# Attention of a vision layer: value matmuls over two heads of a key head, probabilities of 16 heads buffered

## The chip, the cores and the metric

One core of one Trainium2 chip runs the whole kernel as one program. The metric is the device time of one execution in microseconds, the median over runs. The kernel before takes 955.35 us (three runs, 954.17 to 960.56).

## What is computed

Thirty-two images of 256 tokens go through one layer: patches are embedded, an attention block with 16 query heads and 4 key heads follows, then a gated feed-forward block whose weights and inputs are rounded to 8 bits. Cut to what matters here:

```python
q = (x @ wq).reshape(Bx, Sx, 16, 16)
k = (x @ wk).reshape(Bx, Sx, 4, 16)
v = (x @ wv).reshape(Bx, Sx, 4, 16)
q, k = _apply_rope(q, cos, sin), _apply_rope(k, cos, sin)
# head h uses the key and value head h % 4
scores = jnp.einsum('bshd,bthd->bhst', q, k) * scale
scores = jnp.where(causal[None, None, :, :], scores, -jnp.inf)
attn = jax.nn.softmax(scores, axis=-1)
out = jnp.einsum('bhst,bthd->bshd', attn, v).reshape(Bx, Sx, Dx)
return out @ wo
```

Since head h uses value head h % 4, heads 4g to 4g + 3 (a group, g = 0 to 3) use the four value heads once each, and head kv of group g and head kv of group g + 1 share one.

## The kernel before

The kernel has three stages: attention over images (up to about 770 us), then gate and up, then down. Only the first is touched. It is written engine by engine, with its order laid down by hand in one function `step(x)` for each engine, and run for x from -2 to 32: six steps written out, twelve loop rounds of two images, and the rest written out. Step x works on four images at once: patch, normalisation and projection of x + 2, row maxima of x + 1, scores, exponentials and values of x, output projection of x - 1. Each engine goes through its own step in order, and engines meet only at semaphores.

In step x TensorE (PE) does, for image x:
- `score_pair(x, i)`, i = 0 to 7 (L547, L549): transposed scores of two heads into PSUM; the causal structure leaves three blocks of 128x128 a head.
- `attend(x, g)`, g = 0 to 3 (L563, L567): the value product of the four heads of group g. The values (`v_aug`, 32 columns for each value head, with a column of ones for the row sums) are the stationary operand, so that four value heads occupy the four column groups of the array; the probabilities move through, 256 columns for the first key block and 128 for the second, all fp32. The result goes to half of an `o_bank`, two groups to a bank.

ScalarE (ACT) takes each pair of scores to probabilities in `exp_pair` (L865), into `probs`, a buffer of eight heads, and copies a full `o_bank` out in `o_copy` (L873). GpSimd (POOL) zeroes the upper triangle of the diagonal blocks in `mask` (L1013), once for each pair. VectorE (DVE) reduces row maxima of image x + 1 (`reduce_pair`, L1223) as PE delivers them (`unit_pair`, L525 and L532), and works on the normalisation (L1244 to L1264), on `xn_low` (L1297), `max_turned` (L1214) and on the output side.

What waits for what around the change: attend(x, g) waits for masks up to 2g + 1 (`masked`), and for `o_copied` when it begins a bank; exp_pair(x, i) for even i waits for `pv_done`, the attend that last read its half of `probs`; o_copy waits for the two attends of its bank; `values` (L818) for the attends of the image that used the same `v_aug`. In PE's step the order is: patch 0, attend(x - 1, 3), stack_turn 1, patch 1, score 0, stack_turn 2, max_turn 0 and 1, score 1, o_turn 0, unit 0, score 2, o_turn 1, x_turn, stack_turn 0, score 3, unit 1, attend(x, 0), project 0, score 4, unit 2, project 1, score 5, on_turn, unit 3, attend(x, 1), score 6, unit 4, out_project, score 7, unit 5, attend(x, 2). In matmul lines: patch is L454, stack_turn L509, max_turn L491, o_turn L578, x_turn L467, project L479, on_turn L587, out_project L598.

POOL's step is: power, masks 0 to 3, x_low (L1051), mask 4, rotate_cross (L1032), mask 5, rotate (L1021), mask 6, add_rotated (L1046), mask 7, power. rotate_cross waits for both `projected` (L811) of ACT, which wait for project 0 and 1 of PE.

Of the kernel before, what the change touches and what calls it, by code (L numbers as in the profile page):

```python
# [26 lines left out]
P = 128  # L27
# [3 lines left out]
D = 256  # L31
# [89 lines left out]
def vit_layer(nc, x_t, w_emb, w_qkv, w_o, w_gate, w_up, w_down, clips, rope, eye, tri, out):  # L121
    with ExitStack() as ctx:
# [64 lines left out]
        probs = part(8 * 4 * P).rearrange("p (h k s) -> p h k s", h=8, k=4)  # L187
        diagonals = probs.rearrange("p h (a b) s -> p (h a) b s", a=2)[:, :, 0, :]
# [23 lines left out]
        gate_q = ffn[:, 2 * IM * D:5 * IM * D // 2].bitcast(BF16).rearrange("p (m e) -> p m e", m=IM)  # L212
        up_q = ffn[:, 5 * IM * D // 2:3 * IM * D].bitcast(BF16).rearrange("p (m e) -> p m e", m=IM)
        down_n = part(DC * I).rearrange("p (c i) -> p c i", c=DC)
        down_q = part(DC * I, BF16).rearrange("p (c i) -> p c i", c=DC)
        w_inv = part(2 * IM + DC)
        down_diag = part(DC * P).rearrange("p (c h) -> p c h", c=DC)
# [207 lines left out]
        def _(pe):  # L425
# [127 lines left out]
            def attend(x, g):  # L553
                pe.wait_ge(masked, x.n * 8 + (2 * g + 2))
                if g == 0:
                    pe.wait_ge(v_ready, x.n + 1)
                if g % 2 == 0:
                    wait(pe, o_copied, x.n * 2 + (g // 2 - 1))
                cols = (g % 2) * TOKENS
                b = o_bank[g // 2]  # L560
                v = v_aug[x.parity]
                for kv in range(KV):
                    pe.matmul(b[32 * kv:32 * kv + 32, cols:cols + TOKENS], v[:, 0, kv, :],  # L563
                              probs[:, 4 * (g % 2) + kv, 0:2, :], start=True, stop=False,
                              skip_group_check=True)
                for kv in range(KV):
                    mm = pe.matmul(b[32 * kv:32 * kv + 32, cols + P:cols + TOKENS], v[:, 1, kv, :],  # L567
                                   probs[:, 4 * (g % 2) + kv, 2, :], start=False, stop=True,
                                   skip_group_check=True)
# [64 lines left out]
            def step(x):  # L634
# [4 lines left out]
                if w:  # L639
                    attend(x + -1, 3)  # L640
# [30 lines left out]
                if X:  # L671
                    attend(x, 0)
# [16 lines left out]
                if X:  # L689
                    attend(x, 1)  # L690
# [11 lines left out]
                if X:  # L702
                    attend(x, 2)
# [78 lines left out]
        def _(act):  # L782
# [31 lines left out]
            def values(x):  # L814
                y = x + 1
                act.wait_ge(read["qkv"], y.n * 2 + 2)
                wait(act, pv_done, y.n * 4 - 4)
# [42 lines left out]
            def exp_pair(x, i):  # L860
                act.wait_ge(scored, x.n * PAIRS_S + (i + 1))
                if i % 2 == 0:
                    wait(act, pv_done, x.n * 4 + (i // 2 - 1))
                o = 2 * i % 8
# [691 lines left out]
```

## Time and profile before

| | |
|---|---|
| median of three runs | 955.35 us |
| profiled execution, its device time | 954.55 us |
| its span, first to last instruction | 952.8 us |
| mean granted TensorE clock | 0.971 |
| PE busy | 820.2 us, 86% |
| DVE busy | 732.7 us, 77% |
| ACT busy | 621.8 us, 65% |
| POOL busy | 520.0 us, 55% |
| L563, 1024 instructions | 82.7 us |
| L567, 1024 instructions | 51.9 us |
| L1223, 192 instructions | 235.1 us |

Busy time is the time in which at least one instruction of the group runs. Matmuls overlap on PE, so the distance from one start to the next tells more about their cost than their durations. A wait in brackets is idle time of the engine ahead of a row, with the engine, tile and line that ended it.

### The profile page before, as it was taken

Reading aid. Unit: us, or ns where it says so; the run is one execution under the profiler, and the core shown is the slowest. Engines: PE = TensorE matmul, PEld = TensorE weight load, DVE = VectorE, ACT = ScalarE, POOL = GpSimd, SP = SyncE. Lnnn points to the kernel's source line nnn. Section 1 sums busy time; section 2 is a strip of 40 time slices with the busy share of each in tenths; the row PEclk is TensorE's granted clock in tenths of the full one; section 3 lists DMA queues with packets and bytes.
Section 4 is the critical chain, followed back from the end, with each engine's and each line's share of the span. In section 5 each row is a group of like instructions: output and inputs, shape, how many; then the busy total and the mean of one; then the engine's idle time right before and its main releaser. Section 6 shows DMA issues by size and latency. Waiting matters only on the chain. (4 is left out here: it accounts for less than half of the span.)

```text
span 952.8 us, 25805 instructions
## 1 busy us (share of the span) xinstructions
PE 820.2 (86%) x8942; PEld 480.8 (50%) x8942; DVE 732.7 (77%) x1309; ACT 621.8 (65%) x972; POOL 520.0 (55%) x545
## 2 busy tenths in 40 slices
PE   2689999999999999999999999999997849997775
PEld 2345555555555555555555555555554433332443
DVE  5856777777777777777777777777777758999898
ACT  3266666666666666666666666666676537886664
POOL 1456666555666566666666665655565326884000
PEclk9789999999999999999999999999999888998899
DMA  7000111111111111111111111111100011322488
GB/s 268 29 2 2 51 57 51 41 39 39 39 39 39 39 39 39 39 39 39 39 39 39 39 50 49 55 39 39 39 13 12 13 43 36 56 44 67 148 261 251
DMA packets 50052, 54.59 MB, mean 57 GB/s; under 512 B 18912, under 2 KB 45280, under 8 KB 50016
## 3 DMA queue, kind: packets, MB, share of 16 engines
q1 hardware_dynamic: 50016, 54.11, 18.8%
q8 instruction: 22, 0.36, 0.1%
q14 instruction: 14, 0.11, 0.0%
HBM read 33.13 MB, written 16.78 MB: 52 GB/s over the span
## 5 line engine op out<-in xcount | busy, mean ns | idle before, releaser
L1223 DVE TENSOR_REDUCE act_all<-pair 128x8 f32<-128x1024 f32 x192 | 235.1, 1225 | 98.6 <-PE pair L532 98.0
L865 ACT ACTIVATE act_all<-pair 128x768 f32<-128x768 f32 x256 | 207.9, 812 | 133.2 <-PE pair L549 133.2
L1013 POOL TENSOR_SCALAR_AFFINE_SELECT act_all<-act_all 128x512 f32<-128x512 f32 x256 | 162.6, 640 | 100.5 <-ACT act_all L865 100.4
L1056 POOL TENSOR_TENSOR act_all<-act_all 128x2 f32<-128x2 f32 x64 | 60.8, 950 | 210.5 <-DVE act_all L1256 139.9
L454 PE MATMUL pair<-act_all 128*128 128x256 f16 (+1 forms) x960 | 118.4, 277 | 9.4 <-DVE act_all L1158 9.4
L857 ACT ACTIVATE act_all<-pair 128x1024 f16<-128x1024 f16 x64 | 65.7, 1027 | 76.7 <-PE pair L509 76.7
L454 PEld LDWEIGHTS pair<-act_all 128*128 128x128 f16 (+1 forms) x960 | 91.5, 99 | 26.6 <-issue 15.4
L525 PE MATMUL pair<-act_all,eye_b 128*128 128x512 bf16 x256 | 78.5, 389 | 26.6 <-DVE act_all L1223 25.9
L563 PE MATMUL pair<-act_all 128*32 128x256 f32 x1024 | 82.7, 395 | 1.3 <-POOL act_all L1013 1.3
L1051 POOL TENSOR_TENSOR act_all<-act_all 128x1280 f16<-128x1280 f32 x31 | 80.9, 2611 | 1.3 <-ACT act_all L795 1.3
L532 PEld LDWEIGHTS pair<-act_all 32*128 32x128 f16 x1536 | 43.4, 93 | 67.3 <-issue 66.0
L532 PE MATMUL pair<-act_all 32*128 32x128 f16 x1536 | 76.6, 218 | 0.8 <-DVE act_all L1223 0.8
L547 PE MATMUL pair<-act_all 64*128 64x256 f16 x512 | 73.1, 282 | 4.3 <-ACT act_all L857 2.2
L479 PE MATMUL pair<-act_all 128*128 128x384 f16 x384 | 75.6, 335 | 1.5 <-DVE act_all L1297 1.5
L974 ACT ACTIVATE ffn<-pair,gate_scale 128x512 f32<-128x512 f32 x96 | 60.9, 654 | 16.2 <-PE pair L730 9.1
L770 PE MATMUL pair<-wd_t,act_all 128*128 128x256 bf16 (+1 forms) x384 | 46.7, 279 | 20.4 <-ACT act_all L997 20.4
L1032 POOL TENSOR_TENSOR act_all<-act_all 128x320 f32<-128x320 f32 x64 | 53.9, 865 | 17.4 <-ACT act_all L811 17.4
L549 PE MATMUL pair<-act_all 64*128 64x128 f16 x512 | 56.7, 218 | 0.0
L730 PE MATMUL pair<-ffn,wg_t 128*128 128x512 bf16 x160 | 49.1, 389 | 7.3 <-DMA ffn<-ffn 6.2
L578 PE MATMUL pair<-act_all 128*128 128x128 f32 x256 | 42.1, 288 | 14.7 <-DVE act_all L1214 13.9
L509 PE MATMUL pair<-act_all 128*128 128x128 f16 x640 | 52.8, 222 | 1.0 <-DVE act_all L1280 0.8
L1113 POOL TENSOR_TENSOR act_all<-ffn 128x512 f32<-128x512 f32 x32 | 40.7, 1273 | 22.1 <-ACT ffn L962 22.1
(133 smaller groups left out, 1625.9 us busy)
## 6 DMA issues: line engine op xcount, KB each, us to landing
act_all<-x_t SPq DMA_DIRECT2D x32, 640.0 KB, 4.0
out<-act_all SPq DMA_DIRECT2D x32, 256.0 KB, 2.2
ffn<-out SPq DMA_DIRECT2D x16, 512.0 KB, 4.6
out<-ffn SPq DMA_DIRECT2D x16, 512.0 KB, 3.2
act_all<-w_down SPq DMA_DIRECT2D x1, 704.0 KB, 8.4
act_all<-w_emb SPq DMA_DIRECT2D x1, 640.0 KB, 4.0
ffn<-w_gate SPq DMA_DIRECT2D x1, 640.0 KB, 7.1
ffn<-w_up SPq DMA_DIRECT2D x1, 640.0 KB, 7.6
```

Source lines behind the costliest of these rows:

```text
L454: mm = pe.matmul(b[:, 0:D], xs[0:k, sx, c, tb * P:(tb + 1) * P], we[0:k, sw, c, :], start=(c == 0 and (sx, sw) == PARTS[0]), stop=(c == KC ...
L479: mm = pe.matmul(b[:, 0:QKV_COLS], xn_t[:, sx, c, tb * P:(tb + 1) * P], wqkv[:, sw, c, :], start=(c == 0 and (sx, sw) == PARTS[0]), stop=( ...
L525: pe.matmul(max_bank[j], eye_b[:, :], tri_b.rearrange("p (a t) -> p a t", a=1).to_broadcast([P, GROUPS, P]), start=True, stop=False, skip_ ...
L532: mm = pe.matmul(max_bank[j][:, g * P:(g + 1) * P], max_op[rows, g, qt * P:(qt + 1) * P], max_op[rows, 4, kt * P:(kt + 1) * P], start=(qt ...
L547: pe.matmul(b[:, 0:TOKENS], k[rows, kp, 0:P], q[rows, i, :], start=True, stop=True)
L563: pe.matmul(b[32 * kv:32 * kv + 32, cols:cols + TOKENS], v[:, 0, kv, :], probs[:, 4 * (g % 2) + kv, 0:2, :], start=True, stop=False, skip_ ...
L857: act.activation(q_op[y.parity][:, 4 * (k - 1):4 * k, :].rearrange("p g t -> p (g t)"), max_bank[k - 1][:, :].bitcast(FP16), ACT.Copy).the ...
L865: act.activation(probs[:, o:o + 2, 0:3, :].rearrange("p h k s -> p h (k s)"), pair[1][:, :].rearrange("p (h c) -> p h c", h=2)[:, :, 0:3 * P],
L974: act.activation(silu[m % 3][:, 0:cols], bank[2 + m % 3][:, 0:cols], ACT.Silu, scale=gate_scale[:, m:m + 1]).then_inc(silu_ready, 1)
L1013: pool.affine_select(out=p, in_=p, pattern=[[0, 4], [1, P]], compare_op=ALU.is_ge, fill=0.0, base=0, channel_multiplier=-1).then_inc(maske ...
L1051: pool.tensor_tensor(x_parts[v.parity][:, 1], xt[v.parity], x_parts[v.parity][:, 0], ALU.subtract).then_inc(x_low_ready, 1)
L1223: dve.tensor_reduce(to.rearrange("p (g k) -> p k g", g=GROUPS)[:, first:first + 2, :], pair[2][:, :].rearrange("p (k g t) -> p k g t", k=2 ...
```

## The change

`probs` becomes two buffers of eight heads, so all 16 heads of an image have a place: pairs 0 to 3 in the first, pairs 4 to 7 in the second, which lies in the `ffn` tile. attend(x, half) now handles eight heads: each matmul takes the same value head for two groups, 512 columns for the first key block and 2 x 128 for the second, and fills a whole `o_bank`. It is called twice an image: half 0 where attend(x, 1) stood, half 1 where attend(x - 1, 3) stood. The calls for attend(x, 0) and attend(x, 2) are gone. The waits follow: `pv_done` counts two for an image instead of four, attend waits for four or eight masks, exp_pair waits for pv_done only at i = 0 and 4. The feed-forward weights' small buffers change places with the part of `ffn` that is now used.

```diff
-        probs = part(8 * 4 * P).rearrange("p (h k s) -> p h k s", h=8, k=4)
+        probs = [t.rearrange("p (h k s) -> p h k s", h=8, k=4) for t in (part(8 * 4 * P), ffn[:, 0:8 * 4 * P])]
...
-        gate_q = ffn[:, 2 * IM * D:5 * IM * D // 2].bitcast(BF16).rearrange("p (m e) -> p m e", m=IM)
-        up_q = ffn[:, 5 * IM * D // 2:3 * IM * D].bitcast(BF16).rearrange("p (m e) -> p m e", m=IM)
+        gate_q, up_q = (part(IM * D, BF16).rearrange("p (m e) -> p m e", m=IM) for _ in range(2))
...
-            def attend(x, g):
-                pe.wait_ge(masked, x.n * 8 + (2 * g + 2))
-                if g == 0:
+            def attend(x, half):
+
+                pe.wait_ge(masked, x.n * 8 + (4 * half + 4))
+                if half == 0:
                     pe.wait_ge(v_ready, x.n + 1)
-                if g % 2 == 0:
-                    wait(pe, o_copied, x.n * 2 + (g // 2 - 1))
-                cols = (g % 2) * TOKENS
-                b = o_bank[g // 2]
+                wait(pe, o_copied, x.n * 2 + (half - 1))
+                b = o_bank[half]
                 v = v_aug[x.parity]
+                p = probs[half].rearrange("p (g h) k s -> p g h k s", g=2)
                 for kv in range(KV):
-                    pe.matmul(b[32 * kv:32 * kv + 32, cols:cols + TOKENS], v[:, 0, kv, :],
-                              probs[:, 4 * (g % 2) + kv, 0:2, :], start=True, stop=False,
+                    pe.matmul(b[32 * kv:32 * kv + 32, :].rearrange("p (g t) -> p g t", g=2), v[:, 0, kv, :],
+                              p[:, :, kv, 0:2, :].rearrange("p g k s -> p g (k s)"), start=True, stop=False,
                               skip_group_check=True)
                 for kv in range(KV):
-                    mm = pe.matmul(b[32 * kv:32 * kv + 32, cols + P:cols + TOKENS], v[:, 1, kv, :],
-                                   probs[:, 4 * (g % 2) + kv, 2, :], start=False, stop=True,
+                    mm = pe.matmul(b[32 * kv:32 * kv + 32, :].rearrange("p (g t) -> p g t", g=2)[:, :, P:TOKENS],
+                                   v[:, 1, kv, :], p[:, :, kv, 2, :], start=False, stop=True,
                                    skip_group_check=True)
...
-                    attend(x + -1, 3)
+                    attend(x + -1, 1)
...
-                if X:
-                    attend(x, 0)
                 if z:
                     project(x, 0)
...
-                    attend(x, 1)
+                    attend(x, 0)
                     score_pair(x, 6)
...
-                if X:
-                    attend(x, 2)
...
-                wait(act, pv_done, y.n * 4 - 4)
+                wait(act, pv_done, y.n * 2 - 2)
...
-                if i % 2 == 0:
-                    wait(act, pv_done, x.n * 4 + (i // 2 - 1))
-                o = 2 * i % 8
-                act.activation(probs[:, o:o + 2, 0:3, :].rearrange("p h k s -> p h (k s)"),
+                if i % 4 == 0:
+                    wait(act, pv_done, x.n * 2 + (i // 4 - 1))
+                o = 2 * (i % 4)
+                act.activation(probs[i // 4][:, o:o + 2, 0:3, :].rearrange("p h k s -> p h (k s)"),
...
-                act.wait_ge(pv_done, img.n * 4 + (2 * b + 2))
+                act.wait_ge(pv_done, img.n * 2 + (b + 1))
```

First place: PE's queue in the middle of a step, from unit_pair(x, 1) to the second project. L525 and L532 are unit_pair, L563 and L567 attend, L479 project, L547 and L549 score_pair. Before:

```order
L525 MATMUL pair<-act_all,eye_b 128x512 [waits unit_reduced]
L525 MATMUL pair<-act_all,eye_b 128x512
L532 MATMUL pair<-act_all 128x128 x8
L563 MATMUL pair<-act_all 32x256 [waits o_copied,v_ready,masked]
L563 MATMUL pair<-act_all 32x256 x3
L567 MATMUL pair<-act_all 32x128 x4
L479 MATMUL pair<-act_all 128x384 [waits x_t_read]
L479 MATMUL pair<-act_all 128x384 x5
```

The same place now:

```order
L525 MATMUL pair2<-act_all,eye_b 128x512 [waits unit_reduced]
L525 MATMUL pair2<-act_all,eye_b 128x512
L532 MATMUL pair2<-act_all 128x128 x8
L479 MATMUL pair0<-act_all 128x384 [waits x_t_read]
L479 MATMUL pair0<-act_all 128x384 x5
```

attend(x, 0) is gone from here, with its waits, and project follows unit_pair at once.

Second place: PE's queue from unit_pair(x, 5) over the end of the step to stack_turn 1 of the next (L454 is patch 0, L509 stack_turn). Before:

```order
L532 MATMUL pair<-act_all 128x128 x8
L563 MATMUL pair<-act_all 32x256 [waits o_copied,masked]
L563 MATMUL pair<-act_all 32x256 x3
L567 MATMUL pair<-act_all 32x128 x4
L454 MATMUL pair<-act_all 128x256 [waits x_low_ready,x_high_ready,on_t_read]
L454 MATMUL pair<-act_all 128x256 x14
L563 MATMUL pair<-act_all 32x256 [waits masked]
L563 MATMUL pair<-act_all 32x256 x3
L567 MATMUL pair<-act_all 32x128 x4
L509 MATMUL pair<-act_all 128x128 [waits max_ready,stack_high]
```

The same place now:

```order
L532 MATMUL pair2<-act_all 128x128 x8
L454 MATMUL pair0<-act_all 128x256 [waits x_low_ready,x_high_ready,on_t_read]
L454 MATMUL pair0<-act_all 128x256 x14
L563 MATMUL pair3<-ffn,act_all 32x512 [waits o_copied,masked]
L563 MATMUL pair3<-ffn,act_all 32x512 x3
L567 MATMUL pair3<-ffn,act_all 32x2x128 x4
L509 MATMUL pair2<-act_all 128x128 [waits max_ready,stack_high]
```

The attend ahead of patch is gone, and the one behind it has matmuls of 512 and 2 x 128 columns and reads the second buffer.

Third place: PE's queue from unit_pair(x, 3) to unit_pair(x, 4). Now:

```order
L532 MATMUL pair2<-act_all 128x128 [waits unit_reduced]
L532 MATMUL pair2<-act_all 128x128 x7
L563 MATMUL pair3<-act_all 32x512 [waits o_copied,v_ready,masked]
L563 MATMUL pair3<-act_all 32x512 x3
L567 MATMUL pair3<-act_all 32x2x128 x4
L547 MATMUL pair1<-act_all 128x256 [waits exp_done]
```

Nothing has moved past anything here; the attend between them is the doubled one, where before it had 256 and 128 columns.

## Rows read from the trace of the kernel before

**Rows 1.** Busy time in a window: length, then PE, PEld, DVE, ACT, POOL, clock, DMA, GB/s
```profile
84.50:717.21 632.71, 584.50 (x7057) 354.34 (x7057) 480.66 (x953) 429.38 (x701) 393.26 (x420) 1.00 0.12 40
```
**Rows 2.** Waits from 90 to 720 us: who for whom, total us, times, longest
```profile
ACT act_all L865 <- PE pair L549: 113.2, 107, 1.8
...
PE pair L525 <- DVE act_all L1223: 20.5, 56, 0.5
...
PE pair L467 <- DVE act_all L1264: 14.9, 28, 0.5
...
PE pair L578 <- DVE act_all L1214: 12.8, 28, 0.8
```
**Rows 3.** Timeline of PE in one image: start, us, engine, line, shapes, count [wait]
```profile
401.00 0.60 PE L525 MATMUL pair<-act_all,eye_b 128*128 128x512 bf16 x2 [0.46 <-DVE act_all L1223]
401.54 0.40 PE L532 MATMUL pair<-act_all 32*128 32x128 f16 x8
401.86 0.64 PE L563 MATMUL pair<-act_all 128*32 128x256 f32 x8
402.32 0.40 PE L567 MATMUL pair<-act_all 128*32 128x128 f32 x8
402.65 1.15 PE L479 MATMUL pair<-act_all 128*128 128x384 f16 x6
...
403.85 0.22 PE L549 MATMUL pair<-act_all 64*128 64x128 f16 x2
404.00 0.40 PE L532 MATMUL pair<-act_all 32*128 32x128 f16 x8
404.33 1.15 PE L479 MATMUL pair<-act_all 128*128 128x384 f16 x6
...
407.50 0.22 PE L549 MATMUL pair<-act_all 64*128 64x128 f16 x2
407.99 0.61 PE L525 MATMUL pair<-act_all,eye_b 128*128 128x512 bf16 x2 [0.27 <-DVE act_all L1223]
...
413.94 0.64 PE L563 MATMUL pair<-act_all 128*32 128x256 f32 x8
```
**Rows 4.** Timeline of PE inside one attend, its passes, from narrow windows
```profile
406.60 0.42 PE L563 MATMUL pair<-act_all 128*32 128x256 f32 x4
...
406.84 0.40 PE L563 MATMUL pair<-act_all 128*32 128x256 f32 x4
407.05 0.40 PE L567 MATMUL pair<-act_all 128*32 128x128 f32 x8
```
**Rows 5.** Timeline of DVE and POOL in the same image
```profile
401.25 0.69 DVE L1297 TENSOR_TENSOR act_all<-pair,act_all 128x512 f16<-128x512 f32 x1 [0.31 <-ACT act_all L801]
...
401.97 1.23 DVE L1223 TENSOR_REDUCE act_all<-pair 128x8 f32<-128x1024 f32 x1
...
402.09 0.63 POOL L1013 TENSOR_SCALAR_AFFINE_SELECT act_all<-act_all 128x512 f32<-128x512 f32 x1 [2.23 <-ACT act_all L865]
...
406.09 1.68 POOL L1032 TENSOR_TENSOR act_all<-act_all 128x320 f32<-128x320 f32 x2 [0.21 <-ACT act_all L811]
...
406.71 1.23 DVE L1223 TENSOR_REDUCE act_all<-pair 128x8 f32<-128x1024 f32 x1 [1.04 <-PE pair L532]
...
411.91 0.64 POOL L1013 TENSOR_SCALAR_AFFINE_SELECT act_all<-act_all 128x512 f32<-128x512 f32 x1
```
**Rows 6.** Timeline of PE in the last three images
```profile
728.82 0.64 PE L563 MATMUL pair<-act_all 128*32 128x256 f32 x8 [0.34 <-POOL act_all L1013]
...
740.48 0.40 PE L532 MATMUL pair<-act_all 32*128 32x128 f16 x8 [0.36 <-DVE act_all L1223]
...
755.80 1.08 PE L563 MATMUL pair<-act_all 128*32 128x256 f32 x8
...
766.40 0.64 PE L563 MATMUL pair<-act_all 128*32 128x256 f32 x8 [0.92 <-POOL act_all L1013]
```
**Rows 7.** Durations of one line in the whole run: ns least/median/greatest
```profile
L1013 POOL TENSOR_SCALAR_AFFINE_SELECT act_all<-act_all x256: 627/635/954, 59.0 to 765.7; 128x512 f32<-128x512 f32 x128
```

More of the change, by code:

```diff
@@ L184, in vit_layer @@
         v_aug = [part(TB * KV * 32).rearrange("p (b h d) -> p b h d", b=TB, h=KV) for _ in range(2)]
-        probs = part(8 * 4 * P).rearrange("p (h k s) -> p h k s", h=8, k=4)
-        diagonals = probs.rearrange("p h (a b) s -> p (h a) b s", a=2)[:, :, 0, :]
+        probs = [t.rearrange("p (h k s) -> p h k s", h=8, k=4) for t in (part(8 * 4 * P), ffn[:, 0:8 * 4 * P])]
+        diagonals = [p.rearrange("p h (a b) s -> p (h a) b s", a=2)[:, :, 0, :] for p in probs]
         o_sb = part(GROUPS * TOKENS).rearrange("p (g t) -> p g t", g=GROUPS)
@@ L211, in vit_layer @@
         up_n = ffn[:, IM * D:2 * IM * D].rearrange("p (m e) -> p m e", m=IM)
-        gate_q = ffn[:, 2 * IM * D:5 * IM * D // 2].bitcast(BF16).rearrange("p (m e) -> p m e", m=IM)
-        up_q = ffn[:, 5 * IM * D // 2:3 * IM * D].bitcast(BF16).rearrange("p (m e) -> p m e", m=IM)
+        gate_q, up_q = (part(IM * D, BF16).rearrange("p (m e) -> p m e", m=IM) for _ in range(2))
         down_n = part(DC * I).rearrange("p (c i) -> p c i", c=DC)
-        down_q = part(DC * I, BF16).rearrange("p (c i) -> p c i", c=DC)
+        down_q = ffn[:, 4096:4096 + DC * I // 2].bitcast(BF16).rearrange("p (c i) -> p c i", c=DC)
         w_inv = part(2 * IM + DC)
-        down_diag = part(DC * P).rearrange("p (c h) -> p c h", c=DC)
+        down_diag = ffn[:, 4096 + DC * I // 2:4096 + DC * (I // 2 + P)].rearrange("p (c h) -> p c h", c=DC)
         ones = part(P)
@@ L1011, in mask @@
                 fence(pool)
-                p = diagonals[:, 4 * (r % 4):4 * (r % 4) + 4, :]
+                p = diagonals[r // 4][:, 4 * (r % 4):4 * (r % 4) + 4, :]
                 pool.affine_select(out=p, in_=p, pattern=[[0, 4], [1, P]], compare_op=ALU.is_ge,
```

## The prediction

> **What bounds the kernel now.** I start with the busy sums, because they say which engine can set the pace at all. From L525 at 84.50 to the L525 that stands 28 images later the period is 632.71/28 = 22.60 us an image, and TensorE (PE) is busy for 584.50 of the 632.71 us, 92%, at a granted clock of 1.00, that is 2.4 GHz; VectorE (DVE) is busy 76%, ScalarE (ACT) 68%, GpSimd (POOL) 62% [rows 1]. So PE's own work is the period, apart from about 1.7 us of waits an image. The list of waits says where these are: four places, each waiting for DVE, in each image alike. L525 waits for the reduction L1223 twice (20.5 us over 28 images, 0.73 an image: 0.46 at 401.00 and 0.27 at 407.99), L467 for L1264 (0.53) and L578 for L1214 (0.46) [rows 2, 3]. The reader is to see in the timeline of PE that everything else stands back to back. Work taken off PE therefore counts in full as long as no other engine is late at the next wait, and work added just ahead of a wait is free up to the size of that wait. That is the whole argument; what follows is a walk through one image with a clock in hand, from L525 at 401.00 on.
>
> **The price of one attend.** Before, an attend starts at 401.86 and the next work (L479) starts at 402.65: 0.79 us. Its first half (L563 to L567) is 0.46, the second, with the way out, 0.33 [rows 3]. Inside, the trace shows two passes for each matmul (x8 for four written, 1024 for 512 in the run): passes of 256 columns start at 406.60 and 406.84, and L567 starts at 407.05 [rows 4]. So the second pass takes 0.21 us for 256 columns, with four column groups of the array side by side. Four passes of streaming (256, 256, 128, 128 columns) are then 0.21 + 0.21 + 0.11 + 0.11 = 0.64, and 0.15 is fixed for one attend. Is the fixed part really lost with the attend, or does it stay with the neighbours? L532 takes 0.32 before an attend (401.54 to 401.86) and 0.33 before L479 (404.00 to 404.33) [rows 3]: the neighbour costs the same without it, so a removed attend gives back its 0.79.
>
> **The doubled attend.** No row shows 512 fp32 columns in one matmul. From below its price is streaming alone, 1.28; from above twice the old attend, 1.58. I take 1.43 = 2 x 0.64 + 0.15, because what the two pieces of 0.21 and 0.24 us show is a pace by columns with one small start. The output of L567 now has two runs of 128 columns, and its input has two runs far apart; for that I add nothing, and the upper end stands for it. The TensorE page of the Trainium skill ("TensorE: Matmul & The Clock Gate", Back-to-back issue gap) gives a warm matmul a fixed cost of only about 2.5 ns beyond its columns; by that rule merging saves next to nothing, a doubled attend costs nearly the upper end, and the sum would be that of the first rival below. No row here shows that figure by itself, and the 0.15 us above speaks against its use here.
>
> **The walk.** Times are those of the image shown.
>
> First, attend(x, 0) leaves the place behind unit_pair(x, 1). project (L479) could start at 401.86 instead of 402.65, but it needs xn_low, which DVE ends at 401.25 + 0.69 = 401.94 [rows 5]; DVE's result is used about 0.05 later, so 402.00. Gain 0.65. The next unit_pair would start at 403.35; it needs the reduction of 401.97 + 1.23 = 403.20, used at 403.25 [rows 5]. Nothing is lost, but only 0.10 is left.
>
> Second, attend(x, 1) becomes the doubled attend(x, 0): +0.64. It asks for masks 0 to 3, the last of which ends at 402.09 + 0.63 = 402.72, over 3 us before it [rows 5]. Behind it come score_pair(x, 6) and then L525, which before waited: after an L549 the next work comes 0.15 later when nothing is late (403.85 to 404.00); this one started at 407.50, so PE was ready at 407.65 and began at 407.99, 0.34 late [rows 3]. The reduction it waited for starts when unit_pair(x, 3) is through (406.71), ahead of the attend, and doesn't move against it [rows 5]. The extra 0.64 thus fills the 0.34 and costs 0.30. After two steps PE is 0.35 ahead.
>
> Third, attend(x, 2) leaves the end of the step: 0.79 gained. Fourth, the old attend(x, 3) at 413.94 is now the doubled attend(x, 1): 0.64 lost. It starts at 413.94 - 0.35 - 0.79 = 412.80 and asks for mask 7. It ends at 411.91 + 0.64 = 412.55 [rows 5]. POOL works on end from mask 3 to there, with one wait of 0.21 ahead of L1032, for the second projected [rows 5]. PE brings that 0.65 earlier, so the 0.21 goes and mask 7 ends at 412.34: 0.4 of slack where there was 1.4.
>
> The sum for an image: -0.65 + 0.30 - 0.79 + 0.64 = -0.50 us; 0.30 of it is the fixed part of two attends, 0.20 is what the moved places do with waits. I go on with 0.49, as the second decimals of the starts allow no more. The rest of the way (stack_turn, the second patch, both embedded, L1244, L1214, L1264, the reduction) hangs on PE's stack_turn and patch by the waits in the code and moves as one piece, so the three waits of 0.46, 0.53 and 0.46 stay. ACT and DVE see the same work. ACT loses one wait on pv_done in two; none of these was ever the last, since every wait of L865 in the list is for PE's L549 [rows 2]. The moved weight buffers and masks of another tile change no instruction's size, so 0.
>
> How many images? Steps with a patch behind them: images 0 to 28, 29 x 0.49 = 14.2 us.
>
> The last three images differ: no patch separates the last attends. At 728.82 PE already waits 0.34 for POOL's mask, and at 766.40 it waits 0.92 [rows 6]; now 1.43 us of attend stand behind that mask instead of 0.79. Image 29: the mask comes 0.2 earlier and the attend ends 0.64 later, +0.44. Image 30: the place freed by attend(x, 0) is swallowed by a reduction (wait of 0.36 [rows 6]), the two doubled attends cost 0.37 and 0.4: +0.8. Image 31: partly at the lower of PE's two clocks (L563 shows 1.08 for 0.64 at 755.80 [rows 6]) I take -0.5 for attend(x, 0), whose place the exponentials' wait takes over in part, +1.2 for the first doubled attend at that clock (0.64 x 1.08/0.64, rounded up for the way out) and +0.64 for the second, behind the wait for the mask: +1.3. These three are the roughest numbers of the sum. Together +2.5, with 1 and 3.5 as its ends.
>
> The profiled execution: 954.55 - 14.2 + 2.5 = 942.85. It lies 0.80 below the median of the runs shown, 955.35, so the forecast in median terms is 943.7 us, 1.2% less. (About 1% is what a measurement of this kernel can tell from no change.)
>
> **Rivals.**
> *Merging saves no time on PE.* If the fixed 0.15 belongs to each matmul's columns after all, a doubled attend costs 1.58, and an image gives -0.65 + 0.45 - 0.79 + 0.79 = -0.20: 5.8 us, less a tail of 3.2 (2.5 and five attends of 0.15). That is 954.55 - 2.6 + 0.80 = 952.7, within 1%. For it speaks that 512 fp32 columns stand in no row; against it the 0.21 of the pure pass [rows 4]. The rule cited above from the Trainium skill ("TensorE: Matmul & The Clock Gate") comes out here.
>
> *The first gap isn't closed.* With attend(x, 0) gone nothing covers the chain reduction, xn_low, reduction. Its slack is 0.10; if DVE, or ACT's L801 ahead of xn_low, is 0.25 us later than in the rows, the first gain is 0.40 to 0.50 and the image gives about 0.27 us: 29 x 0.27 - 2.5 = 5.3, so 954.55 - 5.3 + 0.80 = 950. For it: 0.10 is thin. Against it: PE's waits for DVE repeat from image to image, with longest ones of 0.5 us where the mean is 0.46 and 0.53 [rows 2].
>
> *Slower: mask 7 comes too late.* attend(x, 1) holds back PE, and patch, stack_turn and ACT's L857 queue behind it. It decides from the point where mask 7 ends 0.4 + 0.49 = 0.9 us later than computed. L1013 lasts 635 ns as a rule and 954 at most [rows 7]; were all five masks of the chain that long, mask 7 would come 1.6 later, PE would wait 1.2, and an image would be 0.7 us longer than before: +20 us with the tail on top, 978. Only something that slows POOL in every image would do it, and the 0.21 ahead of L1032 shows POOL with a little room.
>
> *The change doesn't do what it says* isn't open: the halved count of attends is written down in the order.
>
> **From cases to numbers.** The forecast has 0.6 (own range 940 to 946, down to the sum without the tail and the clock's scatter), the merge without a saving 0.2, the open first gap 0.14, the late mask 0.06. Faster by over 1% (below 945.8) is the first case, 0.6; within 1% the next two, 0.34; slower 0.06. The range goes from 940 to 953 and leaves out the last case and a little on the low side.
>
> **What the new profile would show.** L563 would have 512 instructions of 512 columns; the distance from its start to the next work would be 1.43 (right) or 1.58 (the first rival). L479 would show a wait of about 0.14 for L1297. The wait of 0.27 at L525 would be gone, the three of 0.45 to 0.52 would be there. The doubled attend in front of stack_turn would show no wait for POOL; one there is the slower rival. The period would be 22.1 us. A period of 22.3 to 22.4 with an attend of 1.43 would mean that I've missed a wait.

## The result and the profile after

The changed kernel takes 945.65 us in the median of 15 runs (944.16 to 950.83); the kernel before takes 954.49 us (15 runs). The ratio is 0.9912, with a 95% interval of 0.9893 to 0.9930: 0.9% faster, where 1.2% had been forecast (943.7 us), inside the range of 940 to 953, and by the ratio just inside the band of 1% to which the forecast had given a chance of 0.34, against 0.6 for more. Counted by its border of 945.8 us, which was worked out from the median of 955.35, it lies 0.15 us on the other side. A second set of five runs, beside the last experiments, gave 945.15 us and a ratio of 0.9904 (0.9889 to 0.9919). The profiled execution takes 945.95 us with a span of 944.2, against 954.55 and 952.8.

The changed kernel has other line numbers from ScalarE's part on: L1223 is now L1219 (the reduction), L1297 is L1293 (xn_low), L1264 is L1260, L1214 is L1210, L1013 is L1009 (mask), L1032 is L1028, L865 is L861, L857 is L853. PE's lines are the same.

First the busy time in a window that answers to [rows 1]: length, then PE, PEld, DVE, ACT, POOL, granted clock, DMA share, GB/s.

```profile
85.48:706.59 621.11, 575.85 (x6160) 331.34 (x6161) 480.59 (x953) 429.36 (x701) 392.88 (x420) 1.00 0.13 41
```

The same 28 images take 621.11 us instead of 632.71, 22.18 instead of 22.60 an image. DVE, ACT and POOL are busy for what they were busy before, to 0.5 us; PE has lost 8.65 us of work, and 2.95 us of idle time have gone too. The waits (who for whom, total, times, longest; 90 to 720 us) answer to [rows 2]:

```profile
ACT ffn L861 <- PE pair L549: 103.4, 86, 1.4
...
PE pair L467 <- DVE act_all L1260: 15.1, 28, 0.5
...
PE pair L525 <- DVE act_all L1219: 13.0, 28, 0.5
PE pair L578 <- DVE act_all L1210: 12.7, 28, 0.8
...
PE pair L479 <- DVE act_all L1293: 4.2, 26, 0.2
```

L525 now waits once an image, not twice (28 for 56), and L479 has a new wait of 0.16. The timeline of one image (start, us, engine, line, shapes, count, wait) answers to [rows 3] and [rows 5]:

```profile
396.17 0.60 PE L525 MATMUL pair<-act_all,eye_b 128*128 128x512 bf16 x2 [0.46 <-DVE act_all L1219]
396.42 0.69 DVE L1293 TENSOR_TENSOR act_all<-pair,act_all 128x512 f16<-128x512 f32 x1 [0.31 <-ACT act_all L797]
396.71 0.40 PE L532 MATMUL pair<-act_all 32*128 32x128 f16 x8
...
397.26 1.14 PE L479 MATMUL pair<-act_all 128*128 128x384 f16 x6 [0.16 <-DVE act_all L1293]
...
398.60 0.40 PE L532 MATMUL pair<-act_all 32*128 32x128 f16 x8
...
400.87 0.40 PE L532 MATMUL pair<-act_all 32*128 32x128 f16 x8
...
401.19 1.06 PE L563 MATMUL pair<-act_all 128*32 128x512 f32 x8
...
402.07 0.61 PE L567 MATMUL pair<-act_all 128*32 128x256 f32 x8
...
402.62 0.28 PE L547 MATMUL pair<-act_all 64*128 64x256 f16 x2
...
402.89 0.61 PE L525 MATMUL pair<-act_all,eye_b 128*128 128x512 bf16 x2
...
406.85 0.63 POOL L1009 TENSOR_SCALAR_AFFINE_SELECT ffn<-ffn 128x512 f32<-128x512 f32 x1
...
408.06 1.06 PE L563 MATMUL pair<-ffn,act_all 128*32 128x512 f32 x8
...
409.49 0.62 PE L509 MATMUL pair<-act_all 128*128 128x128 f16 x8
...
418.33 0.60 PE L525 MATMUL pair<-act_all,eye_b 128*128 128x512 bf16 x2 [0.47 <-DVE act_all L1219]
```

The reader is to see four things. The doubled attend takes 402.62 - 401.19 = 1.43 and 409.49 - 408.06 = 1.43 us. From L525 to the L532 of unit_pair(x, 2) it is now 2.43 us; it was 3.00 [rows 3]: 0.57 gained. From unit_pair(x, 3) at 400.87 to L525 at 402.89 it is 2.02 with no wait; 0.30 dearer than before. And mask 7 ends at 407.48, the attend that needs it starts at 408.06.

### The profile page after: what moved, and what is told of

Its sections match the earlier page's. It is cut to its first block and busy times, and to the rows that moved or that the text cites. A ratio compares the mean times of both kernels' runs of the same rounds, so it can differ in the third digit from the quotient of the medians.

```text
span 944.2 us, 23705 instructions
## 1 busy us (share of the span) xinstructions
PE 811.6 (86%) x7918; PEld 453.9 (48%) x7918; DVE 732.7 (78%) x1309; ACT 621.7 (66%) x972; POOL 519.3 (55%) x545
## 5 line engine op out<-in xcount | busy, mean ns | idle before, releaser
L1219 DVE TENSOR_REDUCE act_all<-pair 128x8 f32<-128x1024 f32 x192 | 235.1, 1224 | 93.2 <-PE pair L532 92.4
L861 ACT ACTIVATE ffn<-pair 128x768 f32<-128x768 f32 x128 | 103.7, 810 | 117.1 <-PE pair L549 117.1
L1009 POOL TENSOR_SCALAR_AFFINE_SELECT act_all<-act_all 128x512 f32<-128x512 f32 x128 | 81.2, 645 | 84.6 <-ACT act_all L861 84.5
L454 PE MATMUL pair<-act_all 128*128 128x256 f16 (+1 forms) x960 | 118.9, 278 | 9.5 <-DVE act_all L1154 9.5
L853 ACT ACTIVATE act_all<-pair 128x1024 f16<-128x1024 f16 x64 | 65.7, 1027 | 73.4 <-PE pair L509 73.4
L861 ACT ACTIVATE act_all<-pair 128x768 f32<-128x768 f32 x128 | 104.3, 815 | 7.4 <-PE pair L549 5.6
L454 PEld LDWEIGHTS pair<-act_all 128*128 128x128 f16 (+1 forms) x960 | 91.8, 100 | 24.5 <-issue 10.0
L525 PE MATMUL pair<-act_all,eye_b 128*128 128x512 bf16 x256 | 78.9, 391 | 18.1 <-DVE act_all L1219 17.5
L1009 POOL TENSOR_SCALAR_AFFINE_SELECT ffn<-ffn 128x512 f32<-128x512 f32 x128 | 81.4, 636 | 16.9 <-ACT ffn L861 16.9
L479 PE MATMUL pair<-act_all 128*128 128x384 f16 x384 | 75.8, 335 | 6.6 <-DVE act_all L1293 6.5
L532 PE MATMUL pair<-act_all 32*128 32x128 f16 x1536 | 76.9, 219 | 1.9 <-DVE act_all L1219 1.8
L547 PE MATMUL pair<-act_all 64*128 64x256 f16 x512 | 73.0, 282 | 5.2 <-ACT act_all L853 2.2
L532 PEld LDWEIGHTS pair<-act_all 32*128 32x128 f16 x1536 | 43.7, 93 | 69.1 <-issue 65.4
L1028 POOL TENSOR_TENSOR act_all<-act_all 128x320 f32<-128x320 f32 x64 | 53.7, 861 | 12.2 <-ACT act_all L807 12.2
L549 PE MATMUL pair<-act_all 64*128 64x128 f16 x512 | 56.6, 218 | 0.0
L547 PEld LDWEIGHTS pair<-act_all 64*128 64x128 f16 x512 | 24.6, 93 | 63.4 <-issue 47.1
L578 PE MATMUL pair<-act_all 128*128 128x128 f32 x256 | 42.1, 288 | 14.2 <-DVE act_all L1210 13.4
```

The lines of the kernel that those rows point to most:

```text
L454: mm = pe.matmul(b[:, 0:D], xs[0:k, sx, c, tb * P:(tb + 1) * P], we[0:k, sw, c, :], start=(c == 0 and (sx, sw) == PARTS[0]), stop=(c == KC ...
L479: mm = pe.matmul(b[:, 0:QKV_COLS], xn_t[:, sx, c, tb * P:(tb + 1) * P], wqkv[:, sw, c, :], start=(c == 0 and (sx, sw) == PARTS[0]), stop=( ...
L525: pe.matmul(max_bank[j], eye_b[:, :], tri_b.rearrange("p (a t) -> p a t", a=1).to_broadcast([P, GROUPS, P]), start=True, stop=False, skip_ ...
L532: mm = pe.matmul(max_bank[j][:, g * P:(g + 1) * P], max_op[rows, g, qt * P:(qt + 1) * P], max_op[rows, 4, kt * P:(kt + 1) * P], start=(qt ...
L547: pe.matmul(b[:, 0:TOKENS], k[rows, kp, 0:P], q[rows, i, :], start=True, stop=True)
L853: act.activation(q_op[y.parity][:, 4 * (k - 1):4 * k, :].rearrange("p g t -> p (g t)"), max_bank[k - 1][:, :].bitcast(FP16), ACT.Copy).the ...
```

## The experiments

Each kernel is compared with the kernel before on the same chip. Periods are read from PE's timeline in the same way in all of them: from the first L479 in the step of image 1 to that in the step of image 28, divided by 27. The step of image 29 is the last that has an L479; what comes behind it is called the end below.

| kernel | median us | ratio (95% interval) | period us |
|---|---|---|---|
| before | 954.5 to 955.0 | 1 | 22.61 |
| changed | 945.65, again 945.15 | 0.9912 (0.9893 to 0.9930), 0.9904 (0.9889 to 0.9919) | 22.19 |
| e1_buffers | 955.00 | 1.0012 (0.9985 to 1.0038) | 22.61 |
| e2_places | 945.67 | 0.9904 (0.9867 to 0.9941) | 22.21 |
| e3_first | 949.10 | 0.9948 (0.9924 to 0.9972) | 22.34 |
| e4_second | 951.00 | 0.9972 (0.9951 to 0.9992) | 22.46 |
| e5_tail | 943.79 | 0.9884 (0.9866 to 0.9901) | 22.19 |
| e6_fill | 938.31 | 0.9828 (0.9809 to 0.9846) | 21.90 |
| e7_fill_tail | 936.83 | 0.9802 (0.9778 to 0.9826) | 21.90 |
| e8_pool_after | 955.82 | 1.0000 (0.9978 to 1.0022) | 22.52 |
| e9_pool_before | 958.35 | 1.0034 (1.0016 to 1.0052) | 22.64 |

All but e9 start from the changed kernel. For e1 to e7 its attend takes a third argument, the groups it handles; with one group the matmuls have 256 and 128 columns as before, and pv_done is raised only by the second group of a half.

### e1_buffers: the buffers without the merge

```diff
-                    attend(x + -1, 1)
+                    attend(x + -1, 1, (1,))
...
                     unit_pair(x, 1)
+                if X:
+                    attend(x, 0, (0,))
...
-                    attend(x, 0)
+                    attend(x, 0, (1,))
...
                     unit_pair(x, 5)
+                if X:
+                    attend(x, 1, (0,))
```

> Two buffers of probabilities as in the changed kernel, but four attends an image at their old places with their old shapes; only the buffering and the waits that follow from it are new. My theory (the gain comes from PE's own work and its places, not from the buffering): no change, period 22.60 us an image, 953 to 956 us, L479 without a wait, L525's waits of 0.46 and 0.27 unchanged. Rival (the second buffer lets exponentials and masks run earlier, and that is part of the gain): a shorter period, 22.4 or less, and 950 us or less.

955.00 us, ratio 1.0012, period 22.61, the waits of 0.46 and 0.27 where they were. Sixteen heads' worth of buffer does nothing for time by itself. It only makes the later steps possible.

### e2_places: the places without the long matmul

```diff
-                    attend(x + -1, 1)
+                    attend(x + -1, 1, (0,))
+                    attend(x + -1, 1, (1,))
...
-                    attend(x, 0)
+                    attend(x, 0, (0,))
+                    attend(x, 0, (1,))
                     score_pair(x, 6)
```

> Two buffers, two places as in the changed kernel, but at each place two attends of 256 and 128 columns one behind the other instead of one of 512 and 256. It tells what the 0.15 us beside the streaming belong to. Theory A (to every attend): a place costs 1.58 us from its first L563-type matmul to the next work, the image -0.57 + 0.45 - 0.79 + 0.79 = -0.12, period 22.48, about 953 us with the ends of the run. Theory B (to entering and leaving a run of matmuls on four column groups, whatever their length): a place costs 1.43 to 1.46, period 22.2, about 946 us, as the changed kernel; then the long matmul itself is worth nothing and the place everything.

945.67 us and a period of 22.21: the whole gain, without a single long matmul. Its timeline of PE at one place:

```profile
400.38 0.40 PE L532 MATMUL pair<-act_all 32*128 32x128 f16 x8
400.71 0.64 PE L565 MATMUL pair<-act_all 128*32 128x256 f32 x8
401.16 0.40 PE L570 MATMUL pair<-act_all 128*32 128x128 f32 x8
401.38 0.61 PE L565 MATMUL pair<-act_all 128*32 128x256 f32 x8
401.81 0.40 PE L570 MATMUL pair<-act_all 128*32 128x128 f32 x8
402.15 0.28 PE L547 MATMUL pair<-act_all 64*128 64x256 f16 x2
```

The first attend goes over into the second 0.22 us after its last eight matmuls start (401.16 to 401.38), which is what their columns take. The second needs 0.34 for the same step, because other work follows (401.81 to 402.15). So 0.12 of the fixed 0.15 us belongs neither to the matmul nor to the attend but to leaving a run of matmuls on four column groups, and 0.02 to entering it (0.45 us from the first L565 to L570 in the first attend, 0.43 in the second); theory B holds. Merging proper is worth 1.44 - 1.43 = 0.01 us a place. The Trainium skill ("TensorEngine Tiling (Array Packing)", Key Properties) says that changing the tiling mode drains TensorE, while changing tiles within a mode doesn't; the trace agrees, with 0.34 against 0.22 us.

The work behind the attend differs from it in two things, the tiling and the type (fp16 for fp32). Two other places in the changed kernel's image tell them apart. From L578 to L525 only the type changes, from L491 to L547 only the tiling (narrow windows, the last matmul of a group and the first of the next):

```profile
414.24 0.27 PE L578 MATMUL pair<-act_all 128*128 128x128 f32 x1
414.35 0.38 PE L525 MATMUL pair<-act_all,eye_b 128*128 128x512 bf16 x1
...
412.91 0.22 PE L491 MATMUL pair<-act_all 128*128 128x128 f16 x1
413.08 0.28 PE L547 MATMUL pair<-act_all 64*128 64x256 f16 x2
```

L525 comes 0.11 behind the last L578, which is also the distance within that group (414.02 to 414.24 for two), so the change of type costs nothing. L547 comes 0.17 behind the last L491, whose ten stand 0.056 apart (412.41 to 412.91 for nine): 0.12 again. So the change of tiling costs, with and without column groups. It fits this that L532 took the same before an attend and before L479 in the forecast's walk: either way PE leaves the 32x128 tiling, and taking the attend from between them leaves one change where there were two.

### e3_first and e4_second: one half each

e3_first keeps the doubled attend(x, 0) and puts groups 2 and 3 back at the two old places of the second half; e4_second keeps the doubled attend(x, 1) and puts groups 0 and 1 back.

```diff
 e3_first
-                    attend(x + -1, 1)
+                    attend(x + -1, 1, (1,))
...
                     unit_pair(x, 5)
+                if X:
+                    attend(x, 1, (0,))
 e4_second
                     unit_pair(x, 1)
+                if X:
+                    attend(x, 0, (0,))
...
-                    attend(x, 0)
+                    attend(x, 0, (1,))
```

> Only the first half is merged (attend over groups 0 and 1 behind unit_pair(x, 3)); groups 2 and 3 stand at their old places with their old shapes. My theory: the image gains 0.57 at the freed place (the trace of the changed kernel has 2.43 us from L525 to the next L532 where it was 3.00) and loses 0.30 ahead of unit_pair(x, 4): period 22.60 - 0.27 = 22.33, 28 images 7.6 us, total 947 to 949. L479 waits 0.16 for DVE. Rival (the two halves depend on each other, through POOL or ACT): period and time as before, or all of the gain here, 22.2.

> Only the second half is merged (groups 2 and 3 ahead of stack_turn); groups 0 and 1 stand at their old places with their old shapes. My theory: -0.79 + 0.64 = -0.15 an image, nothing else moves: period 22.45, 28 images 4.2 us less a dearer end of the run (1 to 2 us), total 951 to 953. Waits of 0.46 and 0.27 at L525 stay and L479 has none. Rival (not additive): period 22.6 or 22.3.

Periods 22.34 and 22.46, that is 0.27 and 0.15 less than before; together 0.42, where the changed kernel has 11.60/28 = 0.41 by the window above. The parts add up, and each is of the size that the walk gives it. In total time e3_first gave 949.10 us, just above what was expected, and e4_second 951.00, at the lower edge. The end (from image 29's first L479 to the last instruction) takes 236.56 us in e3_first, only 233.11 in e4_second, and 233.94 before. So the dearer end of the run shows up with the first half, not with the second, which stands behind the late masks. That is not what I had said; but the granted clock differs too. In the 30 us that begin 20 us behind that L479 its mean is 0.77 in e3_first, 0.94 in e4_second and 0.83 before, so the three ends don't show the price of the order alone.

### e5_tail: the last images in the old order

```diff
-                    attend(x + -1, 1)
+                    if x.known and x.n - 1 >= IMAGES - 3:
+                        attend(x + -1, 1, (1,))
+                    else:
+                        attend(x + -1, 1)
...
+                if X and x.known and x.n >= IMAGES - 2:
+                    attend(x, 0, (0,))
...
-                    attend(x, 0)
+                    if x.known and x.n >= IMAGES - 2:
+                        attend(x, 0, (1,))
+                    else:
+                        attend(x, 0)
...
+                if X and x.known and x.n >= IMAGES - 3:
+                    attend(x, 1, (0,))
```

> The changed kernel once more, beside the two others of this call on the same chip. The step of image 0 began 2.0 us later in its profile than in that of the kernel before, with the same instructions ahead of it. If that is scatter of the TensorE clock in the first 55 us (my theory), the first L525 of image 0's step comes somewhere between 57 and 61 us here; if the change itself delays the start, it is at 60 again. Time 944 to 947 us, period 22.18.

> The changed kernel, but attends of the last images (both halves of 30 and 31, and the second half of 29) at their old four places. My theory: the end of the run (from the last steady L525 on) costs 2.0 us more in the changed kernel than before, because nothing of image x + 2 stands between PE and the late masks there, and the longer attend is behind the wait; with the old places there 1.5 to 2 us come back: 943.5 to 944.5 us. Rival (the end is dearer by the TensorE clock, whatever the order): no change, 945.7.

Both kernels ran side by side: 945.15 and 943.79 us, as expected,, with intervals that overlap (0.9889 to 0.9919, 0.9866 to 0.9901), so the totals alone don't settle it. The traces say more. The end takes 236.7 us in both profiles of the changed kernel, 233.05 in e5_tail. The timeline of PE in image 30, changed kernel:

```profile
728.15 0.22 PE L549 MATMUL pair<-act_all 64*128 64x128 f16 x2
729.51 0.40 PE L532 MATMUL pair<-act_all 32*128 32x128 f16 x8 [1.14 <-DVE act_all L1219]
...
731.23 0.61 PE L532 MATMUL pair<-act_all 32*128 32x128 f16 x8 [0.46 <-DVE act_all L1219]
731.77 1.94 PE L563 MATMUL pair<-act_all 128*32 128x512 f32 x8
733.48 1.06 PE L567 MATMUL pair<-act_all 128*32 128x256 f32 x8
734.47 0.28 PE L547 MATMUL pair<-act_all 64*128 64x256 f16 x2
```

And e5_tail at the same step:

```profile
730.42 0.64 PE L565 MATMUL pair<-act_all 128*32 128x256 f32 x8
...
731.91 0.40 PE L532 MATMUL pair<-act_all 32*128 32x128 f16 x8 [0.36 <-DVE act_all L1233]
...
733.62 0.40 PE L532 MATMUL pair<-act_all 32*128 32x128 f16 x8 [0.24 <-DVE act_all L1233]
733.95 0.64 PE L565 MATMUL pair<-act_all 128*32 128x256 f32 x8
```

Where the attend of group 0 is gone, PE stands idle for 1.14 us, and soon after the doubled attend lasts 734.47 - 731.77 = 2.70 us instead of 1.43. The granted clock of the stretch says why the attend is long. Busy time of PE in windows of the same length from image 29's first L479 on (20, then 30 us; length, PE, clock, DMA, GB/s), the changed kernel, then e5_tail:

```profile
707.46:727.46 20.00, 16.21 (x182) 1.00 0.05 15
727.46:757.46 30.00, 22.12 (x198) 0.77 0.03 9
```

```profile
709.85:729.85 20.00, 16.41 (x198) 1.00 0.05 15
729.85:759.85 30.00, 21.58 (x297) 1.00 0.06 19
```

The clock is 0.77 of 2.4 GHz in the mean over the 30 us, a mixture of its two levels 1.2 and 2.4 GHz, and 1.00 in e5_tail. From the L532 ahead of that attend to its end it is 0.51, nearly all at the lower level; below stand the same 30 us of the kernel before:

```profile
731.23:734.47 3.24, 3.24 (x24) 0.51 0.00 0
...
738.86:768.86 30.00, 23.57 (x283) 0.83 0.06 19
```

From the L532 at 731.23 to the L547 behind the attend it is 3.24 us; at the upper level the same work takes 0.33 + 1.43 = 1.76. So 1.48 us of the end are the price of the low clock at this one place, and my rival for this run (the clock) was right in that. Whether the order decides the clock, by the idle time that it leaves on PE, isn't shown. For it: in the step of image 30 the clock falls in six of the seven profiles in which the place behind unit_pair(x, 1) is free there, and in none of the five in which it is filled. Against it: the seventh, e7_fill_tail, has the same two waits (1.14 ahead of 722.47, 0.46 ahead of 724.19), and its attend behind them takes 0.79 us, at the upper level; in e8_pool_after the clock falls at 737.48, ahead of the wait at this place; and the kernel before keeps the old order through all of the end and has 0.83 in the stretch where e5_tail has 1.00. With the same waits ahead of it in image 31's step (0.20, 1.12, 0.36 and 0.69 us, to 0.01 alike) its clock falls at 753.30, and e5_tail's doesn't.

The changed kernel's second profile also shows what its start is worth. In the first profile the step of image 0 had begun 2.0 us later than before; in the second the L491 of that step starts at 56.45, before at 56.50, in the first at 58.50, and in e1 to e7 between 56.00 and 59.87, with the same instructions ahead of it. Its first L525, of which the expectation spoke, starts at 58.01; before at 58.06, in the first profile at 60.06. The granted clock between 0 and 56 us, before and changed:

```profile
0.00:56.00 56.00, 29.74 (x204) 0.82 0.37 126
```

```profile
0.00:56.00 56.00, 29.96 (x185) 0.76 0.39 126
```

In the second profile of the changed kernel it is 0.82 again. The 2.0 us are scatter, and not an effect of the change.

### e6_fill and e7_fill_tail: a version that beats both

```diff
                 if x.known and x.n == IMAGES:
                     turn_weights(0)
+                if X:
+                    attend(x, 0, (0,))
                 if z:
                     x_turn(x)
...
-                    attend(x, 0)
+                    attend(x, 0, (1,))
                     score_pair(x, 6)
```

> The changed kernel, but half 0 is cut again: group 0 goes ahead of x_turn, where PE waits 0.53 us for DVE, group 1 stays behind unit_pair(x, 3), half 1 stays whole. If the walk by waits is right: behind unit_pair(x, 3) 0.64 less work, of which the wait of 0.34 at L525 comes back, so 0.30 gained; ahead of x_turn 0.79 of work over a wait of 0.53, so 0.26 lost there, but the next wait (L525 for the reduction, 0.47) takes that up, so 0. Period 22.18 - 0.30 = 21.88, total about 937 us. Rival (x_turn and what hangs on it, ACT's L797 and xn_low, are the chain that counts): 0.26 lost, period 22.1, 944 us. Rival by the sum of PE's work alone: one more run of column-group matmuls costs 0.13, period 22.3.

938.31 us, ratio 0.9828, period 21.90 (expected 937 and 21.88). The timeline of PE:

```profile
411.50 0.64 PE L565 MATMUL pair<-act_all 128*32 128x256 f32 x8
411.95 0.41 PE L570 MATMUL pair<-act_all 128*32 128x128 f32 x8
412.29 0.66 PE L467 MATMUL pair<-act_all 128*128 128x128 f32 x4
...
413.65 0.61 PE L525 MATMUL pair<-act_all,eye_b 128*128 128x512 bf16 x2 [0.20 <-DVE act_all L1225]
...
418.68 0.64 PE L565 MATMUL pair<-act_all 128*32 128x256 f32 x8
```

L467 has no wait any more, L525 waits 0.20 for 0.46. That is so in every other image of the middle of the run. In those between, the attend of group 0 waits for GpSimd's mask, and the wait of 0.20 is gone; here in the image ahead of the one shown:

```profile
389.94 0.64 PE L565 MATMUL pair<-act_all 128*32 128x256 f32 x8 [0.38 <-POOL act_all L1015]
```

There are 16 such waits between 90 and 700 us, 5.7 us in all. This kernel has more PE work than the changed one (one way out of the column groups more) and is 0.7% faster (938.31 for 945.15, side by side, with intervals that don't overlap); by PE's work alone it should have been slower. The work stands where PE was idle.

e7_fill_tail is the same with the second halves of the last three images cut as in e5_tail.

> The kernel of e6_fill with half 1 of the last three images cut again and put at its old two places. Both effects are expected to add: 21.88 us an image as in e6_fill, and 1.0 to 1.5 us less at the end: 936.5 to 937.5 us. If the end is governed by the TensorE clock, 938.3 as e6_fill.

936.83 us, ratio 0.9802, 1.5 us less than e6_fill, with the same period, 21.90; the end falls from 237.73 to 234.23 us. The two were timed at different times and their intervals overlap, and in the 30 us that begin 20 us behind image 29's first L479 the clock is 0.89 in e7_fill_tail and 0.77 in e6_fill, so how much of the 3.5 us is the order and how much the clock stays open. By its median this is the fastest version of the study, 2.0% below the kernel before. What is left in the image read are waits of 0.27, 0.44, 0.20 and 0.17 us, all for DVE; in every other image they are 0.53 and 0.27 for DVE and 0.38 for GpSimd's mask at the attend of group 0. So the walk that expected only waits for DVE left out that in its new place this attend can be ahead of its masks.

### e8_pool_after and e9_pool_before: how much slack the masks have

```diff
                 wait(pool, qk_ready, z.n)
+                pool.tensor_tensor(spare, qk_of_qkv[:, :, :, 8:16],
+                                   rope_s[:, 1, :, :, 0:8].to_broadcast([P, TB, QK, 8]), ALU.mult)
                 for half in range(2):
```

> The changed kernel with one more GpSimd product of 0.84 us in each image, into a spare place, ahead of rotate_cross, in the chain that ends with mask 7 (it tests the rival on the slower side; its result is used by nothing). In the changed kernel's trace mask 7 ends at 407.48 and the doubled attend starts at 408.06; with 0.1 for the signal the slack is 0.48. My theory: PE waits 0.36 us for POOL ahead of the attend, each image is that much longer, period 22.54, total 955 to 957 us, a wait of L563 for L1009 in every image. Rival (the slack is larger or the wait is made up later, at the waits for DVE): 946 to 950.

> The kernel before with the same extra product of 0.84 us. There mask 7 ends at 412.55 and its attend starts at 413.94, a slack of 1.3. My theory: nothing changes, 954 to 956 us; together with e8_pool_after this shows that the change has used up slack of GpSimd. Rival (GpSimd's load itself costs, say by access to memory): slower by as much as in e8_pool_after.

e8_pool_after takes 955.82 us with a period of 22.52, 0.33 more than the changed kernel's, and all of the gain is gone. The row it was made for (timeline of POOL and PE, e8_pool_after):

```profile
412.71 0.64 POOL L1010 TENSOR_SCALAR_AFFINE_SELECT ffn<-ffn 128x512 f32<-128x512 f32 x1
...
413.49 1.07 PE L564 MATMUL pair<-ffn,act_all 128*32 128x512 f32 x8 [0.30 <-POOL ffn L1010]
```

The attend starts 0.14 after the mask's end, so the slack in the changed kernel is 408.06 - 407.48 - 0.14 = 0.44; 0.84 less 0.44 would make 0.40, and 0.33 came. In e9_pool_before the period is 22.64, hardly moved, but the total is 958.35, 3.4 us more, where I had expected nothing. About 0.9 us of that stand in the period. In the last images, where no patch covers the masks, the wait of 0.34 [rows 6] is 1.14 there, 0.8 more. The rest, 1.7 us, stands between image 0's L491 and image 1's first L479 (31.38 us for 29.66). The mean clock there is 0.89 for 0.94 before, so it may be the clock as well as the masks; it isn't taken apart. So the statement for the middle of the run holds (the old order could swallow 0.84 us, the new one can't), and for the whole run it was too simple.

## Why the prediction was right, and where it wasn't

**What bounds the kernel, and the price of PE's work.** Right. e1_buffers shows that the buffer is worth nothing, and DVE, ACT and POOL do the same work as before.

**The doubled attend, 1.43 us.** The number was right to the hundredth, the reason wrong, and so the number was in part luck. I had put 0.15 us down to "one attend" and took it as speaking against a small fixed cost per matmul, by which I thought a doubled attend would cost 1.58. e2_places shows that both are true: matmuls of half the length cost 0.01 us more a place, so the fixed cost of a matmul is next to nothing, and two old attends in a row cost 1.44 and not 1.58. What the Trainium skill has ("TensorE: Matmul & The Clock Gate", Back-to-back issue gap), about 2.5 ns for a matmul beyond its columns, agrees with that. The rival "merging saves no time on PE" was right in its premise and wrong in its price. My test of the fixed part (L532 lasts 0.33 before an attend and before L479) showed only that the way in isn't dearer; it couldn't tell an attend from a run of attends.

**First step, -0.65.** Measured -0.57, and this is the term that was mis-sized in every image. I took 0.05 us from the end of DVE's instruction to PE's start, from L525 behind the reduction (418.28 to 418.33 in the new trace). Behind xn_low it is 397.11 to 397.26, 0.15. Before, L467 stood 0.15 behind the end of L1264 (421.76 to 421.91), and I could have read it there. 28 times 0.08 is 2.2 us of the gain that did not come. The rival in which the first gap isn't closed did not come about: 0.57 is more than its 0.40 to 0.50, and the next unit_pair (L532 at 398.60) has no wait.

**Second step, +0.30; third and fourth, -0.15.** Both right: 2.02 for 1.72, and 0.15 in e4_second. The wait at L525 is filled as said, and e3_first gives 0.57 - 0.30 = 0.27.

**Mask 7.** Forecast to end 0.4 before it is used, measured 0.58 before the start, of which 0.14 is the signal. The slower rival did not come about; its turning point was put at 0.9 us of lateness. With 0.84 us of extra work e8_pool_after stands at 955.82, where the kernel before stands, so that turning point is borne out: 0.84 us of lateness brings the kernel back to where it started.

**The end, +2.5.** Near in size, and partly by luck. The forecast counts from the L525 of image 29's step; from there the profiles give +2.0 (237.61 us for 235.59), and from image 29's L479, behind the freed place, +2.8 (236.74 for 233.94). By pieces, from PE's timeline before and changed (an image stands for its step):

| piece | forecast | before | changed | difference |
|---|---|---|---|---|
| image 29's L525 to image 30's | +0.44 | 717.21 to 738.13 | 706.59 to 727.17 | -0.34 |
| to the L509 behind image 30's last attend | +0.8 | to 749.31 | to 740.50 | +2.15 |
| to the L630 just behind image 31's out_project | +1.3 | to 774.86 | to 766.89 | +0.84 |
| to the last instruction | 0 | to 952.8 | to 944.2 | -0.63 |

In image 29 the attend behind the mask starts 10.98 us after that L525 (717.57), where it was 11.61 (728.82): 0.63 earlier and not 0.2, so the longer attend cost nothing there. In image 30 the freed place brought nothing, as the walk had it (L532 waits for the reduction again), and without the 1.48 us of low clock the piece would be +0.67, near the forecast's 0.8. So what the walk left out in image 30 is the clock, which fell under a doubled attend; why it fell there isn't shown. The last piece, in which the change does nothing, has a mean clock of 0.95 for 0.94 before, which may be where its 0.63 us come from.

**The sum.** In the profiled executions: start +2.0 (scatter, up to the L491 of image 0's step), the 28 images of the window above -11.6 where 28 x 0.49 had made -13.7, the two edges of that window (image 0, and the place freed in image 29's step) -1.0 and -0.8, end +2.8; together -8.6. The second profile of the changed kernel has no late start and stands at 944.31 us, 10.2 below the kernel before's. In the forecast's own terms the profiled time is 942.85, + 1.6 (12.6 gained from image 0 to 28 for 14.2), + 2.0 at the start, for which it had no term, - 0.5 at the end: 945.95. So two misses of opposite sign are in it. The chance of 0.6 for more than 1% was a little high: with a forecast of 1.2% and a clock that scatters by 2 us in the first 60, the border was closer than the shares said.

## What to carry to other kernels

Matmuls of one tiling should stand together: the cost to save is the change of tiling, 0.12 us each time at the two places measured here, and not the number of instructions. Once the order is written by hand, look for the engine's waits and move work that is ready onto them: in e6_fill that gained another 0.7% with a little more work on the engine than before. And when a gap is opened, ask what was ready late behind it, with the latency of that very pair of instructions, and what an attend there would cost at the lower clock: 2.70 us for 1.43 in image 30. Work moved forward onto a wait can get ahead of its own inputs, as e6_fill's attend does in every other image.

## What the runs showed of the hardware that I had not expected

- From the end of a DVE instruction to the start of the PE work that waits for it, the profile shows 0.05 us behind the reduction L1219, 0.15 behind L1293, 0.14 behind L1260 (416.52 to 416.66) and 0.13 behind L1210 (413.73 to 413.86), in the image shown. Whether that is a real latency or how the profile sets the end of a reduction isn't settled; for a walk with a clock it is all one.
- Two attends one behind the other cost 1.44 us, one attend 0.79: the second is 0.65, its columns alone.
- fp32 followed by bf16 in the same tiling costs PE nothing (0.11 us, the distance within the group), 128x128 followed by 64x128 in the same type 0.12 us.
- The same instructions, up to the L491 of image 0's step, take from 56.0 to 59.9 us in the profiled executions, with a granted clock in the first 56 us between 0.82 (e1_buffers) and 0.73 (e7_fill_tail). That is 0.4% of the run, nearly half of what the change brings.
